# Piecewise linear feed-forward: two roundings done by ScalarE with a bias that VectorE takes out again

## What is computed

```python
def float2fix(x, mantissa_bits):             # round to multiples of 2^-8
    s = jnp.float32(2.0 ** mantissa_bits)
    return jnp.round(x * s) / s

def pwlin_gelu_basic(x, bits_in, bits_out):  # GELU, linear between 33 knots on [-4, 4], 0.25 apart
    xq = float2fix(x, bits_in)
    y = jnp.interp(xq, _PWL_X, _PWL_Y)
    y = jnp.where(xq > 4.0, xq, jnp.where(xq < -4.0, 0.0, y))
    return float2fix(y, bits_out)

h = float2fix(jnp.einsum('bsd,df->bsf', x, w1) + b1, 8)     # 128 -> 512
h = float2fix(pwlin_gelu_basic(h, 8, 8), 8)
out = float2fix(jnp.einsum('bsf,fd->bsd', h, w2) + b2, 8)   # 512 -> 128
```

## Time and profile before

| | |
|---|---|
| median of three runs | 3722.02 us (3713.61 to 3743.43) |
| time of the profiled execution | 3722.49 us |
| its span | 3720.6 us |
| mean granted clock of TensorE | 0.968 of full |
| busy share of the span: TensorE, VectorE, ScalarE, GpSimd | 94%, 65%, 49%, 30% |
| first bias product of the phase, last statistics of it | about 1235 us, 1524 us |

### The profile page before, as it was taken

One profiled execution on the slowest core, in us unless ns is written; L12 is line 12 of the kernel. 1 busy time (PEld: TensorE's weight loads), 2 busy tenths in 40 slices (PEclk: granted clock), 3 DMA queues, 4 the chain that ended last, 5 costly groups with the idle time before them and its releaser, 6 DMA issues. The chain is left out here.

```text
span 3720.6 us, 101723 instructions
## 1 busy us (share of the span) xinstructions
PE 3508.0 (94%) x44952; PEld 2934.4 (79%) x44952; DVE 2435.8 (65%) x5147; ACT 1816.4 (49%) x3066; POOL 1109.7 (30%) x814
## 2 busy tenths in 40 slices
PE   5999899998999788899999989999999989999999
PEld 4888788886888455688888867778888878888888
DVE  5987555554656799666666656666666666666665
ACT  2544555555656555455555544455555553223332
POOL 1223233334444233222222223322222212222222
PEclk9999999998879899899999989999999999999999
DMA  2000000001000000000000010010000000000000
GB/s 101 10 11 10 2 1 1 1 1 37 14 12 8 7 1 1 8 7 8 7 7 9 4 30 1 1 42 9 7 8 7 9 2 1 12 1 12 1 12 12
DMA packets 14779, 40.47 MB, mean 11 GB/s; under 512 B 3149, under 2 KB 4749, under 8 KB 12814
## 3 DMA queue, kind: packets, MB, share of 16 engines
q1 hardware_dynamic: 14341, 33.97, 2.9%
HBM read 29.77 MB, written 4.19 MB: 9 GB/s over the span
## 5 line engine op out<-in xcount | busy, mean ns | idle before, releaser
L648 ACT ACTIVATE projL<-bank 128x512 f32<-128x512 f32 (+1 forms) x640 | 372.0, 603 | 652.2 <-PE bank L228 636.3
L455 POOL TENSOR_TENSOR probL<-probL,invL 128x1024 f32<-128x1024 f32 x160 | 304.6, 1903 | 1187.0 <-DVE invL L735 1187.0
L1280 POOL TENSOR_TENSOR accM<-accM,partM 128x512 f32<-128x512 f32 x272 | 349.6, 1285 | 771.0 <-DVE partM L1385 768.7
L1355 ACT ACTIVATE siluM<-bank 120x512 f32<-120x512 f32 x240 | 143.4, 598 | 442.2 <-PE bank L228 442.1
L541 PEld LDWEIGHTS bank<-valuesL,probTL 64*64 64x64 f32 x10240 | 280.7, 134 | 68.8 <-issue 54.5
L541 PE MATMUL bank<-valuesL,probTL 64*64 64x128 f32 x10240 | 319.9, 274 | 13.0 <-ACT probTL L658 13.0
L1302 PEld LDWEIGHTS bank<-ahead_second,hM 120*128 120x128 f32 x2560 | 310.5, 192 | 15.0
L724 DVE TENSOR_REDUCE neg_maxL<-bank 128x16 f32<-128x1024 f32 x160 | 195.9, 1225 | 185.1 <-PE bank L560 152.5
L1302 PE MATMUL bank<-ahead_second,hM 120*128 120x128 f32 x2560 | 311.5, 275 | 0.0
L1302 PEld LDWEIGHTS bank<-w2T,hM 128*128 128x128 f32 x2304 | 277.4, 192 | 37.0 <-ACT hM L1358 21.6
L1385 DVE TENSOR_TENSOR partM<-bank,gatesM 128x512 f32<-128x512 f32 x272 | 187.6, 690 | 172.0 <-PE bank L1302 170.2
(11 more groups left out here) (265 smaller groups left out, 8238.6 us busy)
## 6 DMA issues: line engine op xcount, KB each, us to landing
ct0L<-in_ctxP SPq DMA_DIRECT2D x24, 192.0 KB, 2.4
ct1L<-in_ctxP SPq DMA_DIRECT2D x24, 192.0 KB, 2.5
x<-in_x SPq DMA_DIRECT2D x4, 1024.0 KB, 8.8
out<-x SPq DMA_DIRECT2D x4, 1024.0 KB, 3.9
nct<-in_ctxP SPq DMA_DIRECT2D x16, 192.0 KB, 2.4
ahead_second<-in_L0w SPq DMA_DIRECT2D x2, 1152.0 KB, 11.7
ahead_second<-in_L3down SPq DMA_DIRECT2D x1, 1200.0 KB, 15.6
ahead_second<-in_L3gate SPq DMA_DIRECT2D x1, 900.0 KB, 6.6
```

Source lines behind the costliest of these rows:

```text
L455: nc.gpsimd.tensor_tensor(segments(prob[:, slot, :]), segments(prob[:, slot, :]), per_segment(inv[:, slot, :]), ALU.mult).then_inc(prob_re ...
L648: nc.scalar.activation(proj[:, u, :], rot.bank(step, f"P{u}")[0:rows, :], ACT.Copy, scale=scale if paired and u % 2 == 0 else 1.0).then_in ...
L1280: nc.gpsimd.tensor_tensor(acc[:, :, :], acc[:, :, :], part[:, ex % 2, :, :], ALU.add)\
```

## The change

ScalarE now rounds by adding GRID as the bias of an Identity activation (`grid`, a column set by GpSimd): in `on_grid`, which moves from VectorE to ScalarE, and in the new `round_output`. The constant stays in the result. `knot` and `distance` take it out with other constants, and the sum with the stream takes it out of the output (`y_grid`, a second buffer beside `y`).

On ScalarE rounding of the next tile stands between the two lookups of a tile, and round_output of group i - 2 after the lookups of n = 0. On VectorE the order of a step is now knot, weighted, distance, rounded. The output block is split: the bias pass (`add_bias`) stays at n = 3 for group i - 1, and the sum (`add_output`) with take_stats stands at n = 1 for group i - 2. The `Chain` is gone; `y_rounded` and `x_done` are new semaphores.

```diff
--- before.py
+++ after.py
@@ -1611,9 +1611,10 @@
         w1, b1, w2, b2 = sb("pw1", [P, N * P]), sb("pb1", [P, N]), sb("pw2", [P, N, D]), sb("pb2", [P, D])
         shift = sb("pshift", [P, 2])
         hb, u, X = (sb(n, [P, 2, GT]) for n in ("phb", "pu", "pX"))
+        grid = sb("pgrid", [P, 1])
         rest, G0, G1, part, h = (sb(n, [P, N, GT]) for n in ("prest", "pG0", "pG1", "ppart", "ph"))
         four = sb("pfour", [P, P])
-        y = sb("py", [P, G, D])
+        y, y_grid = sb("py", [P, G, D]), sb("py_grid", [P, G, D])
         h_bank, y_bank, o_bank, xt_bank = c.bank[0:2], c.bank[2:4], c.bank[4:6], c.bank[6]
         w_in, shift_set = sem("w_in"), sem("shift_set")
         xh_ready, xt_done, xT_ready = sem("xh_ready"), sem("xt_done"), sem("xT_ready")
@@ -1624,7 +1625,8 @@
         knots, diff_ready, part_ready, y_done, four_set = (
             sem(n) for n in ("knots", "diff_ready", "part_ready", "y_done", "four_set"))
         h_ready, O_done, out_read = (sem(n) for n in ("h_ready", "O_done", "out_read"))
-        chain, bn_done, stats_done = sem("chain"), sem("bn_done"), sem("stats_done")
+        y_rounded, x_done = sem("y_rounded"), sem("x_done")
+        bn_done, stats_done = sem("bn_done"), sem("stats_done")
 
         def before(i, n, lag):
 
@@ -1639,6 +1641,7 @@
 
             @block.gpsimd
             def _(pool):
+                nc.gpsimd.memset(grid[:, :], GRID).then_inc(shift_set, 1)
                 nc.gpsimd.memset(shift[:, 0:1], -QUARTER).then_inc(shift_set, 1)
                 nc.gpsimd.memset(shift[:, 1:2], -QUARTER + 0.25).then_inc(shift_set, 1)
                 for i in range(NG):
@@ -1711,7 +1714,7 @@
                 keep_transposed(nc, act, c, xt_bank, 0, 0, xt_done, xT_ready)
                 scale_group(nc, c, 1, xh_ready)
                 nc.scalar.activation(four[:, :], c.ident[:, :], ACT.Copy, scale=4.0).then_inc(four_set, 1)
-                act.wait_ge(shift_set, 2)
+                act.wait_ge(shift_set, 3)
                 act.wait_ge(w_in, 64)
 
                 def add_bias(i, n):
@@ -1720,12 +1723,25 @@
                     nc.scalar.activation(hb[:, n % 2, :], h_bank[n % 2][:, :], ACT.Identity, bias=b1[:, n:n + 1])\
                         .then_inc(hb_ready, 1)
 
-                def look_up(i, n):
+                def on_grid(i, n):
+
+                    e = i * N + n
+                    act.wait_ge(hb_ready, e + 3)
+                    if e >= 2:
+                        act.wait_ge(rest_ready, e - 1)
+                    nc.scalar.activation(u[:, n % 2, :], hb[:, n % 2, :], ACT.Identity, bias=grid[:, :]).then_inc(u_ready, 1)
+
+                def look_up(i, n, between):
                     e = i * N + n
                     act.wait_ge(X_ready, e + 1)
                     act.wait_ge(y_done, e + 1)
                     nc.scalar.activation(G0[:, n, :], X[:, n % 2, :], ACT.Gelu, bias=shift[:, 0:1])
+                    between()
                     nc.scalar.activation(G1[:, n, :], X[:, n % 2, :], ACT.Gelu, bias=shift[:, 1:2]).then_inc(knots, 1)
+
+                def round_output(i):
+                    act.wait_ge(out_read, i + 3)
+                    nc.scalar.activation(y_grid[:, :, :], y[:, :, :], ACT.Identity, bias=grid[:, :]).then_inc(y_rounded, 1)
 
                 def group(i, slot, first):
                     for n in range(N):
@@ -1735,32 +1751,35 @@
                             add_bias(i + 1, 0)
                         if n == 1:
                             keep_transposed(nc, act, c, xt_bank, i + 1, 1 - slot, xt_done, xT_ready)
-                        look_up(i, n)
+                        if n < N - 1:
+                            look_up(i, n, lambda: on_grid(i, n + 1))
+                        else:
+                            look_up(i, n, lambda: on_grid(i + 1, 0))
+                        if n == 0 and i >= 2:
+                            round_output(i - 2)
                         if n == N - 1 and not (isinstance(i, int) and i == NG - 1):
                             scale_group(nc, c, i + 2, xh_ready)
 
                 add_bias(0, 0)
+                on_grid(0, 0)
                 sweep(group)
+                round_output(NG - 2)
+                round_output(NG - 1)
 
             @block.vector
             def _(dve):
                 scales.compute(dve)
                 dve.wait_ge(w_in, 64)
 
-                def on_grid(i, n):
-                    dve.wait_ge(hb_ready, i * N + n + 3)
-                    nc.vector.tensor_scalar(u[:, n % 2, :], hb[:, n % 2, :], GRID, GRID, ALU.add, ALU.subtract)\
-                        .then_inc(u_ready, 1)
-
                 def knot(i, n):
                     dve.wait_ge(u_ready, i * N + n + 3)
                     dve.wait_ge(knots, i * N + n + 1)
-                    nc.vector.tensor_scalar(X[:, n % 2, :], u[:, n % 2, :], -0.125 + 1.0 / 512, QUARTER, ALU.add, ALU.add)\
+                    nc.vector.tensor_scalar(X[:, n % 2, :], u[:, n % 2, :], -(GRID + 0.125), QUARTER, ALU.add, ALU.add)\
                         .then_inc(X_ready, 1)
 
                 def distance(i, n):
                     dve.wait_ge(X_ready, i * N + n + 1)
-                    nc.vector.scalar_tensor_tensor(out=rest[:, n, :], in0=X[:, n % 2, :], scalar=QUARTER,
+                    nc.vector.scalar_tensor_tensor(out=rest[:, n, :], in0=X[:, n % 2, :], scalar=QUARTER - GRID,
                                                    in1=u[:, n % 2, :], op0=ALU.subtract, op1=ALU.subtract)\
                         .then_inc(rest_ready, 1)
 
@@ -1775,37 +1794,43 @@
                     nc.vector.tensor_scalar(h[:, n, :], y_bank[n % 2][:, :], GRID, GRID, ALU.add, ALU.subtract)\
                         .then_inc(h_ready, 1)
 
-                def add_output(i, slot):
-                    ch = Chain(dve, chain, i, 2)
+                def add_bias(i, slot):
                     dve.wait_ge(O_done, (i + 1) * N + N)
+                    if i > 0:
+                        dve.wait_ge(y_rounded, i)
                     nc.vector.tensor_tensor(y[:, :, :], o_bank[slot][:, :].rearrange("p (t d) -> p t d", t=G),
                                             b2[:, :].unsqueeze(1).to_broadcast([P, G, D]), ALU.add).then_inc(out_read, 1)
-                    dve.wait_ge(out_read, i + 3)
-                    ch.link(nc.vector.tensor_scalar(y[:, :, :], y[:, :, :], GRID, GRID, ALU.add, ALU.subtract))
+
+                def add_output(i):
+                    dve.wait_ge(y_rounded, i + 1)
                     xg = c.x[:, bass.ts(i, G), :]
-                    ch.link(nc.vector.tensor_tensor(xg, y[:, :, :], xg, ALU.add))
-                    ch.close()
+                    nc.vector.scalar_tensor_tensor(out=xg, in0=y_grid[:, :, :], scalar=GRID, in1=xg, op0=ALU.subtract,
+                                                   op1=ALU.add).then_inc(x_done, 1)
+                    dve.wait_ge(x_done, i + 1)
+                    take_stats(nc, dve, c, i, bn_done, stats_done)
 
                 def group(i, slot, first):
                     for n in range(N):
-                        on_grid(i, n)
+                        knot(i, n)
                         if n >= LAG - 1 or not first:
                             weighted(*before(i, n, LAG - 1))
-                        knot(i, n)
+                        distance(i, n)
                         if n >= LAG or not first:
                             rounded(*before(i, n, LAG))
-                        distance(i, n)
+                        if n == 1 and i >= 2:
+                            add_output(i - 2)
                         if n == N - 1 and not first:
-                            add_output(i - 1, 1 - slot)
-                            take_stats(nc, dve, c, i - 1, bn_done, stats_done)
+                            add_bias(i - 1, 1 - slot)
 
                 sweep(group)
                 for n in range(N - LAG, N):
                     if n + 1 < N:
                         weighted(NG - 1, n + 1)
                     rounded(NG - 1, n)
-                add_output(NG - 1, 1)
-                take_stats(nc, dve, c, NG - 1, bn_done, stats_done)
+                    if n == N - LAG:
+                        add_output(NG - 2)
+                add_bias(NG - 1, 1)
+                add_output(NG - 1)
```

## The result

The changed kernel takes 3708.99 us (median of 20 runs, 3683.14 to 3753.36), the kernel before 3743.27 (20 runs, 3713.61 to 3828.18). The ratio is 0.993, with a 95% interval of 0.9902 to 0.9959: some 26 us less, 15 to 37. A second comparison on another chip gave 0.9944 (0.9903 to 0.9985). All ratios here compare only the executions of a kernel within 1.5% of its fastest, which is why 0.993 is nearer to 1 than the ratio of the medians (0.991), and why one execution of the kernel before that took 8346.64 us at a granted clock of 0.455 doesn't count. The kernel is faster, by less than the 43 us forecast and by less than the 1% from which the prediction counts a kernel as faster, and its time lies above the range.

What follows compares the result with a forecast made beforehand. VectorE was fullest and TensorE waited once a group for its weighted difference; afterwards TensorE would be fullest. Middle 38.9 plus tail 4.6 less head 0.2 saves 43.3 us, from 3722 to 3679 us; 8-in-10 range 3664 to 3703.

Steps and rivals of the forecast that it cites:

- The middle: The 14 distances between output blocks: from 240.45 us to 14 x 14.4, saving 38.9 us.
- TensorE's need of 14.32 us: TensorE's products for one group of four tiles, without idle time: three steps of 3.47 us and one of 3.91.
- The clock no longer falls: TensorE's granted clock stays 1.00 in the stage; five long groups each lose their extra 1.69 us, 8.4 in all.
- rival A: VectorE stays the bound, each of four subtractions holding it up 1.06 us: 15.7 us a group, 3697 us; chance 0.18.
- The chain at tile 1: From bias product over ScalarE's copy, lookup and rounding to knot and weighted difference: done at +4.56 us, fitting by 0.2.
- The wait of VectorE for ScalarE once a group: Sign that the forecast is right: VectorE waits for ScalarE's rounding once a group, at the knot of tile 2.
- Most subtractions fall into its slack or beside the rounding from PSUM: GpSimd's subtractions against VectorE's 2.14 us queue in a 3.47 us step: little collision, 14.4 us a group, not 14.32.
- Its sign of a new sum over 1 us: VectorE's sum with the stream, held up by GpSimd, would take over 1 us if VectorE stayed the bound.
- The load of each engine: Busy time a group after the change: VectorE 13.2 or 13.9 us, ScalarE 13.2, TensorE fullest at 14.32.
- The tail: End of the stage: 5.9 us of waiting and slow clock go, 0.9 and 0.4 come, saving 4.6 us.
- The head: Pipeline fill at the start: four new roundings in ScalarE's queue cost between 0 and 2.4 us, 0.2 taken.
- Rivals C and D: Chain over ScalarE's rounding: C, 2 us longer than summed, 3718 us, chance 0.05; D, slower than before, 3760 us, chance 0.05.

Runs made afterwards that it cites:

- e4: Changed kernel with ScalarE's rounding of the next tile ahead of both lookups: 14.31 us between output blocks, phase 253.02 and 254.18 us, ratio to before 0.9892.
- e6: Changed kernel with VectorE's step ordered knot, weighted, rounded, distance: 14.31 us between output blocks, phase 253.69 and 256.17 us, ratio to before 0.9889.
- e7: Kernel before with only the inner rounding moved to ScalarE and VectorE's new step order, output block as before: 18.08 us between output blocks, phase 311.36 us.
- e5: Changed kernel with VectorE's step ordered knot, rounded, weighted, distance: 15.90 us between output blocks, phase 279.57 us.
- e3: Changed kernel with a second full GpSimd subtraction ahead of each one: 17.72 us between output blocks, phase 307.39 us.
- e2: Kernel before with GpSimd's subtraction done on one column of 512 only: 15.06 us between output blocks, phase 262.66 us.
- u1: Changed kernel with the output rounding back on VectorE, output block still split: 15.51 us between output blocks, phase 274.13 us.

## Why the prediction was wrong

**The absolute time.** The forecast started from 3722 us, the median of three runs and the time of an execution whose phase ahead was at the fast end. Over 20 runs before has 3743.27. Those 21 us are most of the 30 between 3679 and 3709; the rest is the phase, which lost 33.35 us and not 43.3. The three runs spread over 30 us, which should have widened the range upward by itself. Neither error would have left the range alone: 3743 less 43.3 is 3700, and 3722 less 33.35 is 3689.

**The middle.** This is the step of the argument that failed, the cost that it gave to GpSimd's subtractions: 38.9 us forecast, 240.45 - 210.21 = 30.2 measured, 15.01 us a group and not 14.4. Of its terms:

- TensorE's need of 14.32 us was right: three kernels run at 14.31.
- The clock no longer falls: right, 1.00 in the whole stretch.
- VectorE's queue: rival A has 11.5 us in it, and measured is 15.01 less 3.7, 11.3. Right.
- The new rounding at 0.71 us: 0.708. Right.
- The chain at tile 1: right to a few hundredths as far as ScalarE goes. From the bias product (1407.26) L207 comes at +1.50, the lookup at +1.99 and the rounding at +2.60, against +1.50, +2.00 and +2.61. The knot came at +3.66 and not +3.40, because the statistics were only just done, at +3.7 and not the +2.3 (held up once +3.3) forecast. The wait of VectorE for ScalarE once a group, which the prediction names as a sign, didn't come.
- "Most subtractions fall into its slack or beside the rounding from PSUM": wrong. It priced four subtractions at 0.1 us a group. All four hit a knot or a distance and cost 3.7. There was no slack for them to fall into, because I took TensorE's pace for given and then looked whether VectorE fits. It did fit in e4 and e6, which differ in one place of the order. The order that was built settles in a rhythm in which VectorE sets the pace and has no slack at all, and nothing in my argument excluded it; why it doesn't fall into the faster one is not shown. The means of L1763, L1770 and L1784 already spoke for 2.7 us a group (44 us over 16 groups, which the prediction rounds to 2.9).

**Rival A** was the right mechanism, at 0.92 us a subtraction instead of its 1.06. It had 0.18. Its sign of a new sum over 1 us didn't come (675 ns): the subtractions caught knot and distance instead.

**The load of each engine** said 13.2 to 13.9 us for VectorE. It kept the standing still of L1763 and L1770, and at most that of L1784, whereas holding up grew from 2.9 to 3.7 us.

**The tail** was right: from the second last output block to the next phase's table load 20.8 us before and 15.9 after, 4.9 less (4.6 forecast). **The head** lost 1.8 us (phase start to first output block 37.1 and 38.9), within 0 to 2.4 but not the 0.2 taken; in the second profile of the changed kernel it lost 2.9. 30.2 + 4.9 - 1.8 is the 33.3 us.

**Rivals C and D** were about this chain, and the mechanism is real: without the split block the kernel is slower than before (e7, 311.36 us). I priced it only for chains longer than my sum, and saw that the block fills the hole, but not that most of the gain hangs on where the block stands.

## What to carry to other kernels

When two engines exclude each other, a feasible schedule at the other engine's pace is no forecast: sum the fuller engine's queue with every exclusion at full price, and take something less only where a row shows the pass that it will start beside. What to do is then cheap: shift an order so that the other engine's instruction runs beside a pass from PSUM. Look at the waits too, though: e5 halved the holding up and lost more by waiting. And before moving work to another engine, look whether the same work, moved in its own queue into a hole of waiting, does it: here that was 29 of 33 us.

## What the runs showed of the hardware

GpSimd's instruction, once ready, may get in between two VectorE passes that stand directly behind each other, or may not. In the changed kernel it went in as the weighted difference ended (1411.26, 1411.87 above). In the kernel before, timeline, it was ready at the same point and let the knot pass, so that it took 2.15 us itself:

```profile
1391.37 2.15 POOL L1647 TENSOR_TENSOR pG<-pG 128x512 f32<-128x512 f32 x1 [5.26 <-ACT pG L1728]
...
1391.37 0.69 DVE L1770 TENSOR_TENSOR ppart<-prest,pG 128x512 f32<-128x512 f32 x1
...
1391.97 0.42 DVE L1758 TENSOR_SCALAR pX<-pu 128x512 f32<-128x512 f32 x1
...
1392.31 0.69 DVE L1775 TENSOR_SCALAR ph<-bank 128x512 f32<-128x512 f32 x1
```

I can't say from these runs what decides it. The passes that read PSUM with one input (L1794) or PSUM and a broadcast row (L1801) took between 670 and 693 ns in all 16 profiles, whatever GpSimd did. This agrees with the Trainium skill (SBUF — State Buffer, Who interferes with whom), by which only two-port passes and those with two SBUF inputs exclude GpSimd's reads.

TensorE's clock fell after waits of 2.0 to 2.5 us, in some groups and not in others (before: 5 of 14; e7: 4 of 14; e3: 4 of 14). In these 14 groups it didn't fall once with waits of half a us in each (e2) or of 1.4 us in every second one (u1).
